# A decoder layer's recurrent mixer on one core: row norm and head copies move to ScalarE, the gate projection and the gating to other places

## The reference, cut to what matters

```python
delta = shifted - x                                   # x: normed rows; shifted: one step earlier
z = tanh((x + delta * mu_x) @ W_x1.T)                 # 5 branches r, w, k, v, g
mus = einsum('blnr,dnr->blnd', z, W_x2) + x_bias
r, k, v, g = ((x + delta * mu) @ W.T for each branch)
w = -exp(tanh((x + delta * w_mu) @ A_w.T) @ B_w.T + b_w)
def step(S, (q, k, v, w)):                            # per head, 100 steps
    kv = outer(k, v)
    o = q @ (S + u * kv)
    S = exp(w) * S + kv
o = groupnorm(o) * gn_weight + gn_bias
out = (o * silu(g)) @ W_o.T
```

## Time and profile before

| | before |
|---|---|
| median of three runs (lowest, highest) | 1471.85 us (1469.97, 1473.28) |
| the profiled execution: its own time / its span | 1473.77 us / 1472.0 us |
| TensorE, VectorE, ScalarE, GpSimd busy, of the span | 90%, 67%, 39%, 50% |
| mean granted TensorE clock | 0.969 |
| mixer | from 0 to 436.69 us |

### The profile page before, as it was taken

How to read it: one execution, slowest core, us unless ns; L and a number is a source line. 1 busy time by engine, 2 the same in 40 slices (tenths; PEclk the granted TensorE clock), 3 DMA queues, 4 the chain that set the end, 5 groups by cost and what they waited for, 6 DMA issues and landing times.

```text
span 1472.0 us, 31054 instructions
## 1 busy us (share of the span) xinstructions
PE 1319.8 (90%) x9852; PEld 888.0 (60%) x9853; DVE 979.2 (67%) x2060; ACT 581.3 (39%) x1423; POOL 738.3 (50%) x1063
## 2 busy tenths in 40 slices
PE   4788888988757999999999999999988999999996
PEld 2456655665544666666666666666655566666664
DVE  3688987798742788888888888888884322222221
ACT  1343334333402555555555555555543221222121
POOL 4223432343215567788777777777863322222222
PEclk9999999999875999999999999999998999999999
DMA  4997000000006555554454545555432333222322
GB/s 142 271 298 195 1 1 1 0 0 2 1 27 96 97 108 127 123 110 114 123 119 123 128 116 121 125 122 125 110 93 64 51 48 46 43 46 45 45 43 22
DMA packets 152750, 127.81 MB, mean 87 GB/s; under 512 B 41630, under 2 KB 145510, under 8 KB 152614
## 3 DMA queue, kind: packets, MB, share of 16 engines
q1 hardware_dynamic: 140310, 112.02, 31.3%
q0 software_dynamic: 12304, 14.10, 6.4%
HBM read 35.90 MB, written 44.83 MB: 55 GB/s over the span
## 4 chain that ended last, share of the span: by engine, by line
PE 55%; DVE 7%; issue 3%; ACT 2%; DMA 1%; SPq 0%; POOL 0%; DVEq 0%; ACTq 0%; POOLq 0%
PE bank_st L1946 10%; PE bank_v L1964 7%; PE bank_s L1778 6%; PE bank_v L1766 6%; PE bank_o L1808 4%; PE bank_st L1788 4%; DVE neg_raw L1467 4%; PE bank_m L1741 4%; PE bank_s L1946 3%; PE bank_m L1830 2%; PE bank_st L1797 2%; DVE bank_st L1478 2%; PE bank_o L1955 2%; PE bank_v L1756 1%; PE bank_m L1818 1%
## 5 line engine op out<-in xcount | busy, mean ns | idle before, releaser
L1467 DVE TENSOR_REDUCE neg_raw<-bank_s 100x2 f32<-100x722 f32 x256 | 229.4, 896 | 30.1 <-PE bank_s L1778 29.9
L1314 ACT ACTIVATE prob<-bank_st 120x400 f32<-120x400 f32 (+1 forms) x384 | 166.2, 514 | 158.6 <-PE bank_st L1797 158.6
L1254 POOL DMA_INDIRECT out<-result,target x57 | 88.3, 1549 | 234.3 <-DVE result L1684 216.8
L1478 DVE TENSOR_SCALAR bank_st<-bank_st 121x1200 f32<-121x1200 f32 x128 | 180.3, 1409 | 1.7 <-PE bank_st L1788 1.1
L1679 DVE TENSOR_TENSOR hidden<-silu,bank_st 128x512 f32<-128x512 f32 x57 | 39.2, 687 | 192.8 <-PE bank_st L1946 192.8
L1946 PE MATMUL bank_st<-expert_w,rows_t 128*128 x344 | 159.5, 600 | 0.6 <-issue 0.5
L745 PE MATMUL bank_l<-q_heads,k 128*100 128x192 f32 (+4 forms) x512 | 118.2, 372 | 26.7 <-DVE attn L558 14.9
L391 ACT ACTIVATE q_heads<-q 32x192 f32<-32x192 f32 (+3 forms) x168 | 62.1, 369 | 193.9 <-DVE q L517 191.0
L1778 PE MATMUL bank_s<-k_st,q_st 96*128 96x361 bf16 x512 | 123.7, 323 | 13.9 <-DVE neg_raw L1467 8.2
L1153 POOL TENSOR_TENSOR neg_diag<-xident_b,neg_max 100x400 bf16<-100x400 bf16 x128 | 109.2, 853 | 47.5 <-DVE neg_max L1472 46.9
L745 PEld LDWEIGHTS bank_l<-q_heads,k 128*100 128x100 f32 x512 | 82.0, 173 | 64.0 <-DVE attn L538 21.2
(11 more groups left out here) (230 smaller groups left out, 2558.9 us busy)
## 6 DMA issues: line engine op xcount, KB each, us to landing
k_st<-k_part SPq DMA_DIRECT2D x384, 90.2 KB
slot_rows<-empty SPq DMA_DIRECT2D x9, 2967.0 KB, 27.6
q_st<-q_part SPq DMA_DIRECT2D x192, 50.0 KB
kv<-in_ctx_t SPq DMA_DIRECT2D x32, 270.8 KB
expert_w<-in_w SPq DMA_DIRECT2D x16, 512.0 KB, 4.1
rows<-slot_rows SPq DMA_DIRECT2D x57, 129.0 KB
residual<-in_w SPq DMA_DIRECT2D x16, 256.0 KB
residual<-in_x SPq DMA_DIRECT2D x8, 400.0 KB
```

The costliest lines, as they stand in the source:

```text
L1314: act.activation(prob[0:KEYS[c], t % 2, c], bank_st[0:KEYS[c], c, 0:4 * T], ACT.Exp).then_inc(exp_done, 1)
L1467: dve.tensor_reduce(neg_raw[:, h:h + 2], bank_s[0:T, :, 0:S], AX.X, ALU.max, negate=True).then_inc(max_done, 1)
L1478: dve.tensor_scalar(tile, tile, CLAMP, -CLAMP, ALU.min, ALU.max).then_inc(clipped, 1)
```

## The change

1. Row norm on ScalarE. GpSimd's `norm` makes also `offset` = -mean * rstd in two more small products (with a constant tile `minus_one`); `norm_apply` is now four ScalarE activations Identity(rstd * x + offset), placed at s = 6 ahead of `front(g + 1, 6)`. VectorE's `norm_apply` is gone.
2. Head copies. ScalarE's `heads` copies all four heads; VectorE's `heads` is gone, and the two semaphores become one.
3. Transposes (piece 0) and piece 1's `delta` and `xz` are made one body earlier, at s = 7 for group g + 2, and the transposes go to banks 2 and 3 (free after the values) instead of 0 and 1.
4. Piece 7, the gate projection, is made for the body's own group: TensorE runs it between two halves of level 0 (batches 0 and 1, then 2 and 3), ScalarE after the copies of level 1, and VectorE makes `gate` at s = 1 behind `head_scale`.
5. GpSimd's `gating` stands behind the mixing sums of branches 0 and 1 of the next group, no more ahead of them.

```diff
@@ pool
             def norm(g):
                 pool.wait_ge(mv_done, (g + 1) * G)
+                after(pool, xn_done, g * G)
                 pool.tensor_tensor(rstd[:], mean_var[:, :, 1], eps[:, 0:G], ALU.add).then_inc(eps_added, 1)
                 pool.wait_ge(eps_added, g + 1)
                 pool.tensor_tensor(rstd[:], rstd[:], power[:, 0:G], ALU.pow).then_inc(rstd_done, 1)
+                pool.wait_ge(rstd_done, g + 1)
+                pool.tensor_tensor(offset[:], mean_var[:, :, 0], rstd[:], ALU.mult).then_inc(scaled_mean, 1)
+                pool.wait_ge(scaled_mean, g + 1)
+                pool.tensor_tensor(offset[:], offset[:], minus_one[:], ALU.mult).then_inc(offset_done, 1)
...
                     head_norm(g - 1)
-                    gating(g - 1, 1 - p)
                 for i in range(BRANCHES):
...
                         mix(g + 1, i)
+                    if i == 1 and not first:
+                        gating(g - 1, 1 - p)
@@ scalar
+            def norm_apply(g):
+                act.wait_ge(offset_done, g + 1)
+                after(act, xn_turned, g * CC)
+                for j in range(G):
+                    row = ...
+                    act.activation(xn[:, j], row, ACT.Identity, bias=offset[:, j:j + 1], scale=rstd[:, j:j + 1]
+                                   ).then_inc(xn_done, 1)
...
-                for h in range(3):
+                for h in range(RH):
...
             heads(0, 0, 0)
+            norm_apply(1)
+            front(1, 1, 0)
...
-                    if more:
+                    if s == 6 and two_more(g):
+                        norm_apply(g + 2)
+                    if s == 7 and two_more(g):
+                        front(g + 2, p, 0)
+                    if s == 0 and not first:
+                        front(g, p, 7)
+                    if more and 0 < s < 7:
                         front(g + 1, 1 - p, s)
@@ vector
-            norm_apply(0)
...
             norm_stats(1)
-            norm_apply(1)
-            heads(0, 0, 0)
+            front(1, 1, 1)
...
-                    if s == 0 and more:
-                        front(g + 1, 1 - p, 1)
...
-                    if s + 1 < LEVELS:
-                        if s >= 1:
-                            decay_q(g, p, s + 1)
-                        heads(g, p, s + 1)
-                        if s >= 1:
-                            decay_k(g, p, s + 1)
-                    elif more:
-                        heads(g + 1, 1 - p, 0)
+                    if 1 <= s < LEVELS - 1:
+                        decay_q(g, p, s + 1)
+                        decay_k(g, p, s + 1)
...
                     if s == 7 and two_more(g):
-                        norm_apply(g + 2)
-                    if more and s > 1:
+                        front(g + 2, p, 1)
+                    if s == 1 and not first:
+                        front(g, p, 7)
+                    if more and 1 < s < 7:
                         front(g + 1, 1 - p, s)
@@ tensor
                 if piece == 0:
-                    after(pe, gate_in, 2 * g)
+                    after(pe, val_done, 2 * g)
...
-                            mm = pe.transpose(bank_f[c][:, j * T:(j + 1) * T], xn[:, j, c * 128:(c + 1) * 128],
+                            mm = pe.transpose(bank_f[2 + c][:, j * T:(j + 1) * T], xn[:, j, c * 128:(c + 1) * 128],
...
                 if piece == 1:
-                    after(pe, val_done, 2 * g)
...
                 if piece == 2:
+                    after(pe, gate_in, 2 * g)
...
+            front(1, 0)
...
-                if more:
-                    front(g + 1, 0)
                 if not first:
                     weigh(g - 1, 1 - p)
                 for s in range(LEVELS):
-                    level(g, p, s)
+                    if s == 0 and not first:
+                        level(g, p, 0, (0, 1))
+                        front(g, 7)
+                        level(g, p, 0, (2, 3))
+                    else:
+                        level(g, p, s)
...
-                    if more and s > 0:
+                    if s == 7 and two_more(g):
+                        front(g + 2, 0)
+                    if more and 0 < s < 7:
                         front(g + 1, s)
```

More of the change, by code:

```diff
@@ L110, in stage_mixer @@
         rstd = sb("rstd", [T, G])
+        offset = sb("offset", [T, G])
         xn = sb("xn", [T, G, D])
@@ L325, in by_batch @@
                 return tile.rearrange("p (b t) -> p b t", b=G)
+            def norm_apply(g):
+                act.wait_ge(offset_done, g + 1)
+                after(act, xn_turned, g * CC)
+                for j in range(G):
+                    row = x1[:, g * G + j, :] if isinstance(g, int) else \
+                        x1[:, bass.ds(g * G + j, 1), :].rearrange("p b d -> p (b d)")
+                    act.activation(xn[:, j], row, ACT.Identity, bias=offset[:, j:j + 1], scale=rstd[:, j:j + 1]
+                                   ).then_inc(xn_done, 1)
             def front(g, p, piece):
@@ L332, in front @@
                         after(act, xz_done, g * CC)
-                        act.activation(xn_t[:, c, :, 1:T + 1], by_batch(bank_f[c][:, 0:GT]),
+                        act.activation(xn_t[:, c, :, 1:T + 1], by_batch(bank_f[2 + c][:, 0:GT]),
                                        ACT.Copy).then_inc(xn_t_done, 1)
@@ L341, in front @@
                     act.wait_ge(r_summed, g + 1)
-                    after(act, heads_act, 3 * LEVELS * (g - 1))
-                    after(act, heads_dve, LEVELS * (g - 1))
+                    after(act, heads_done, RH * LEVELS * (g - 1))
                     act.activation(q[:, p, :, 0:T], by_batch(bank_f[0][:, 0:GT]), ACT.Copy).then_inc(q_done, 1)
@@ L391, in heads @@
                     act.activation(dst, src, ACT.Copy,
-                                   scale=bonus[rows, 0:1] if lv == 0 else 1.0).then_inc(heads_act, 1)
+                                   scale=bonus[rows, 0:1] if lv == 0 else 1.0).then_inc(heads_done, 1)
+            norm_apply(0)
             for piece in range(8):
@@ L444, in norm_stats @@
                 dve.wait_ge(stats_done, (g + 1) * G)
+                after(dve, offset_done, g)
                 dve.sem_inc(waited, 1)
@@ L447, in norm_stats @@
                     dve.bn_aggr(mean_var[:, j], stats[:, j]).then_inc(mv_done, 1)
-            def norm_apply(g):
-                dve.wait_ge(rstd_done, g + 1)
-                after(dve, xn_turned, g * CC)
-                for j in range(G):
-                    dve.tensor_scalar(xn[:, j], rows_of(g, j, 1), mean_var[:, j, 0:1], rstd[:, j:j + 1],
-                                      ALU.subtract, ALU.mult).then_inc(xn_done, 1)
             def front(g, p, piece):
@@ L479, in front @@
                                                  ALU.mult).then_inc(gate_done, 1)
-            def heads(g, p, lv):
-                rows = slice(RK * 3, RK * 4)
-                if lv == 0:
-                    dve.wait_ge(q_done, g + 1)
-                if lv >= 2:
-                    dve.wait_ge(q_decayed, g * (LEVELS - 2) + lv - 1)
-                after(dve, level_summed, G * (LEVELS * g + lv - 1))
-                if lv == 0:
-                    dve.tensor_scalar(q_heads[rows, 0, 3], q[rows, p, :, 0:T], bonus[rows, 0:1], None,
-                                      ALU.mult).then_inc(heads_dve, 1)
-                else:
-                    src = odd(q[rows, p], lv)
-                    dst = q_heads[rows, lv % 2, 3, :, 0:COLS[lv]].rearrange("p b (s h) -> p b s h", s=src.shape[2])
-                    dve.tensor_copy(dst, src).then_inc(heads_dve, 1)
             def seg_views(p, lv):
@@ L724, in front, with level @@
                     project(bank_f[1], w_g[:, :, 128:256], 0, g_summed)
-            def level(g, p, lv):
-                pe.wait_ge(heads_act, 3 * (g * LEVELS + lv + 1))
-                pe.wait_ge(heads_dve, g * LEVELS + lv + 1)
+            def level(g, p, lv, batches=range(G)):
+                pe.wait_ge(heads_done, RH * (g * LEVELS + lv + 1))
                 if lv == 0:
@@ L733, in level @@
                 copied = g * START[LEVELS]
-                for j in range(G):
+                for j in batches:
                     cols = COLS[lv]
```

14 lines of the change are left out of this document (8 added, 6 removed).

## The result

Before 1471.7 us (median of 4 runs on that chip, 1470.0 to 1473.3), after 1452.9 us (median of 4, 1452.5 to 1454.2): ratio 0.987, 95% interval 0.985 to 0.988. The change takes 19 us off. The profiled execution took 1454.2, its span 1452.4.

The account below looks back on a forecast made before the run. No engine is full; TensorE and VectorE, nearly full, hand over to each other in the mixer, whose end moves the total. Shifts summing to -18.4 us from 1473.8 gave 1455.4, placed at 1454.5; own range 1449 to 1460, wider range 1446 to 1465.

Parts of the forecast that it names:

- TensorE's part: From r projection to level 0's third matmul: 31.40 us before, 28.66 forecast (-2.74), of which 1.36 for the diagonal copy's wait.
- VectorE's part: Level 0's third matmul to the next group's first part; its window starts at the third diagonal copy: 13.8 us forecast, +0.6.
- Part to r: From the next group's first part to its r projection: 3.54 us before, 2.62 forecast without gating ahead, -0.92.
- rival A: Contention, with gating stretching VectorE's decays and levels 2 and 3 paying the fourth copy: 1464 us; chance 0.18.
- Period: From one r projection to the next in the loop: 45.10 us forecast against 48.16, -3.06 a group.
- Shift of the r projections: Whole mixer: prologue -1.2, body 0 -3.5, bodies 1 to 5 -15.3, the loop's back jump +0.6 us.
- the fall of the clock around 290 us: Clock at 0.50 for some 7 us, lengthening one period by 1.7; left out, result 1.7 lower if it doesn't return.
- Last body and drain: Mixer's end, no mixing to gain, two head copies less, gate products more: +1.0 us, bounds 0 and +2.
- the head copy of 0.93 us: VectorE's copy that waited on GpSimd's mixing, 0.26 when undisturbed; its removal counted at nothing.
- Rival B: All eight levels wait for ScalarE's longer copies, 3.0 us a period, so nothing is gained: 1472 us; chance 0.05.
- Rival C: Slower: at level 7's end delta and xz wait on the norm chain and hold up VectorE's queue: 1484 us; chance 0.09.
- Rival D: More than forecast: TensorE becomes the bound, its 41.8 us a group; half of the way gives 1443 us; chance 0.08.

Follow-up runs that it names:

- the version without the split: Changed kernel with the w_g projection behind the whole of level 0 instead of between its halves: 1452.8 us, ratio 0.988.
- order: Changed kernel with gating ahead of mixing again, head 3's copies and the row norm back on VectorE: 1473.8 us, ratio 1.000 to the kernel before.
- order and copies, the first experiment: Changed kernel with GpSimd gating ahead of the mixing sums again: 1471.6 us, ratio 1.000 to the kernel before.
- gating moved: Kernel before with only GpSimd's gating moved behind the first two mixing sums: 1473.5 us, ratio 1.001.
- gating and copies: Kernel before with gating moved behind the first two mixing sums and ScalarE copying all four heads: 1463.5 us, ratio 0.994.
- order and gating: Changed kernel with VectorE copying head 3 again, ScalarE three heads: 1465.9 us, ratio 0.996 to the kernel before.
- the last experiment, the better version: Changed kernel with gate products at level 6, w_g behind level 1, both head statistics behind the diagonal copies: 1443.8 us, ratio 0.980.

## Why the prediction was right, and where not

It said 1454.5, and 1452.9 was measured. The mechanism held: TensorE's part and the part from the first part to the r projection get shorter, VectorE's part hardly changes (13.2 before), and the period counts six times. Its steps:

- **TensorE's part**: 28.66 forecast, 28.78 measured (154.07 to 182.85). No wait ahead of the transposes, none at the third matmul.
- **VectorE's part**: 13.8 forecast (1.08 and 12.72, in the sum 12.74), 13.3 measured (1.02 and 12.29). The gate products took 1.05, not 1.2. The fourth copy was put at 0 with 0.8 as the upper end, level 2's heads at 35.4 behind r: they were ready at 35.4. The wait there, 0.93, is no longer than the 1.09 of before, and as the window sets the end it costs nothing: with that wait gone, the version without the split has the same time.
- **Part to r**: 2.62 forecast, 2.70 measured (151.36 to 154.07). Gating beside VectorE cost nothing: in VectorE's rows above, gating lies from 156.00 to 158.23 beside mask copies (1.02) and parts (1.17) that read a bank; 1.04 and 1.31 is what these take elsewhere in the period. So rival A's price for the gating wasn't met. Beside the mixing sums the stretching is there, 1.20 instead of 0.41 for k's decay, but it was there before the change too (1.07). The rule of the Trainium skill that rival A cites (SBUF — State Buffer, "SBUF: two separate sides") has only VectorE operations with two SBUF inputs lock with GpSimd's, or those in a faster mode that takes both ports. This trace agrees with it in both places; I had charged it to a place where VectorE reads PSUM banks.
- **Period**: 45.10 forecast, 44.8 measured: 0.3 too much, 1.5 us in all.
- **Shift of the r projections** (profiled executions): prologue -1.2 forecast, -2.0 measured; body 0 -3.5, -3.8; five periods with the jump -14.7, -17.75. Of the last, 1.7 are the fall of the clock around 290 us that the prediction named and left out: it did not return. The jump cost the forecast +0.6 (46.30 against 44.80, where it was 49.07 against 48.17).
- **Last body and drain**: +1.0 forecast, with +2 as the upper end; +2.97 in the profiled execution (from the last r projection to the mixer's end at 416.12, 81.4 against 78.5), out of bounds. Granted clock and TensorE in the last 23 us of the mixer, after:

```profile
394.00:396.00 2.00, 2.00 (x14) 2.00 (x14) 0.70 (x6) 0.00 (x0) 0.00 (x0) 0.50 0.00 0
```
```profile
393.01 4.92 PE L751 MATMUL bank_t<-val,attn 100*100 100x64 f32 x32 [0.71 <-DVE attn L552]
...
408.63 6.47 PE L769 MATMUL bank_t<-w_o,normed_t 128*100 128x256 f32 x16 [2.26 <-POOL normed_t L308]
```
and before:
```profile
416.00:420.00 4.00, 3.04 (x32) 2.90 (x32) 2.02 (x16) 0.00 (x0) 0.00 (x0) 1.00 0.00 0
```
```profile
416.09 3.04 PE L755 MATMUL bank_t<-val,attn 100*100 100x64 f32 x32 [0.71 <-DVE attn L548]
```

  The last weighing of 32 matmuls took 4.92 at 0.50 (1.2 GHz) instead of 3.04 at full clock, 1.9 us, and the output projection 6.47 instead of 5.83: 2.5 of the 2.97. The new work isn't the reason. The kernel with the row norm on VectorE has the same last body and drain, instruction for instruction, and in its trace they take +0.65 (79.1, mixer's end at 414.43):

```profile
393.85 3.04 PE L749 MATMUL bank_t<-val,attn 100*100 100x64 f32 x32 [0.71 <-DVE attn L546]
...
407.58 5.83 PE L767 MATMUL bank_t<-w_o,normed_t 128*100 128x256 f32 x16 [2.26 <-POOL normed_t L308]
```

  So the forecast's +1.0 was about right for the work, and the rest is when the clock falls in the drain: at 394 us in the one, at 398.6 in the other, at 421 before. Why it falls at one time or the other no run shows.

The profiled execution was to take 1455.4 and took 1454.2. It came 0.8 sooner by the prologue, 0.3 by body 0, 1.3 by the periods and 1.7 by the clock, and later by 2.0 in the drain and 1.0 behind the mixer (1036.3 against 1035.3, code that the change doesn't touch): errors of both signs. That the total is nearer than its terms is luck.

**Where the reasoning was off though the sum held.** The prediction gave each edit an amount of its own: order -2.74 and +1.2 for the gate products, -1.5 together; copies -0.6; gating -0.92. The table has each kernel's period where the clock held, and what it really took. Two entries of the first column rest on less than the others: "order" on the one opening of six at which the clock held, and "order and copies" on none, it is 47.8 less the 1.42 of the r projection:

| kernel | period, clock held | period | total to before, us |
|---|---|---|---|
| before | 48.2 | 48.2 | 0 |
| gating moved | 48.4 | 48.4 | +1 |
| gating and copies | 46.7 | 46.7 | -9 |
| order | 46.3 | 48.0 | 0 |
| order and copies | 46.4 | 47.8 | 0 |
| order and gating | 46.6 | 46.6 | -6 |
| order, gating, copies | 44.8 | 44.8 | -19 |

(The norm and the split were each taken back in the last kernel alone, and moved its period by at most 0.2.) The order is worth 1.8 to 1.9 in any company: 48.2 to 46.3, 48.4 to 46.6, 46.7 to 44.8; forecast 1.5. Gating and copies are worth 1.5 together in either order, the forecast's 0.92 and 0.6, but next to nothing singly: gating alone uncovers level 4's wait behind the copy of 0.93 (seen in both orders); copies alone (with the norm), in the new order, bring part 0.6 sooner and the wait at r grows from 2.4 to 3.05. Copies alone in the old order no run has. The step of the prediction that doesn't hold is the one on VectorE's copies, "so is the head copy of 0.93 us", counted at nothing: its cover was gone as soon as gating was moved, and it is worth 1.0 a group. And the 1.36 given for the filled wait inside level 0 is no gain of the split, since VectorE's part follows either way; it belongs to the whole order.

What no step had is that a wait ahead of the r projection can cost more than its length. Before the change it was 1.67, after 1.41, and the clock held at both; at 2.4 it fell at five of six openings and at 3.05 to 3.53 at all six, for about 1.4 a group. With gating left ahead of the mixing the new order meets this, and so my expectation for the first experiment, 1461, was 10 us too low.

Rival B would have needed levels without slack, and five have it; it failed as foreseen. The rule of the Trainium skill cited under it (Perfetto Trace Analysis, "Optimizing Scalar/DVE Operations"), that a copy for which VectorE has a faster mode is faster there, agrees with the single copy (0.26 against 0.37 us). Keeping one of four copies there costs this kernel 13 us all the same. Rival C's cover was 1.2 us. Rival D was not met, but lay within reach: 43.3 a group in the last experiment.

## What to carry to other kernels

When two engines close a period together, lay it out anew from one fixed event to the next for both, and look at every cover that an edit uses up: an edit that gives nothing alone can be half of a pair (here gating moved alone gave 0, and with the copies 9 us). Look at the granted clock before you call an edit worthless, since a wait that grows can take back the gain by the clock behind it. The stretch in which one engine runs without a gap while the other waits is where moved work pays one for one, if it lands where the other engine has slack.

## What the runs showed of the hardware

- Beside GpSimd's mixing sums VectorE's operations that read and write the SBUF alone are stretched: decays with two inputs took 0.8 to 1.2 us instead of 0.2 to 0.4, the head copy with one input 0.93 instead of 0.26. Those that read a PSUM bank keep their time beside gating (1.02 and 1.17). Which engine pays can change from one group to the next: in the kernel with gating first, VectorE's decays took 0.98 and 1.19 and four mixing sums 4.12 at one opening, 0.23 and 0.43 and 4.40 at another, where the r projection came 0.5 later.
- A ScalarE activation of 256 columns with pointers for scale and bias: 2.07 us for four in a row.
- The granted clock fell to 0.50 behind TensorE's wait at the opening of every full group in one kernel (waits 3.05 to 3.53), at five of six in another (2.4), and at none once the wait was filled with matmuls; where the fall covered the r projection it cost 1.4 us.
- Shorter waits can be followed by a fall too. The three kernels with the old order (before, gating moved, gating and copies moved) each had one fall of 7 us among the full groups, behind the wait of 1.1 to 1.3 ahead of the transposes, in another period each time (287, 189, 140 us); the same wait stands in every period of theirs. Without the split, a wait of 1.93 inside level 0 was followed by one once (183 us, w_g 4.07 instead of 2.85, the period 1.7 longer) and by none in the next two undisturbed periods. The changed kernel, whose waits in the loop are at most 1.41, had none between 60 and 340 us.
- After the loop's jump VectorE's next statistics or diagonal copy starts 1.9 to 2.3 us late, and the wait at the third matmul of level 0 grows: in the changed kernel from 0 to 1.07 (period 46.30 instead of 44.80), in the better version from 0.89 to 3.06, with a fall of the clock behind it.
